# Reordering the front of a three-block language-model tower: warm-up matmuls, statistics one tile ahead, queries before the last values

## The reference

```python
tok = wte[input_ids]
Q = _layer_norm(tok, gamma, beta) @ W_proj.T            # 8 heads of 64
V = (tok @ W_val.T)
Q_store = Q[:, :, :-2, :] * arrow_mask                  # mask: id equals a link id
denom = jnp.maximum(arrow_mask.sum() * H, 1.0)
Q_erase = Q_store / norm(Q_store)
erase = einsum('bhip,bhiq->hpq', Q_erase, Q_erase @ value_traces) / denom
traces = 0.99 * (value_traces - erase) + 0.1 * einsum(Q_store, V_store) / denom
h = (shifted Q @ traces) @ W_out.T
# attention on _layernorm(h)
q, k, v = split(x @ W_qkv + b_qkv)
gw = softmax(gelu(v @ W_gp)); group_weight = gw @ gw.T
attn = softmax(q @ k.T * scale * group_weight)
out = ((1 - a) * attn + a * group_weight) @ v @ W_proj + b_proj
# then the experts on _layernorm(h)
```

## Time and profile before

| | us |
|---|---|
| median of 3 runs | 470.39 |
| lowest, highest | 470.22, 473.29 |
| the profiled execution | 471.55 |
| its span, first to last instruction | 469.7 |
| PE, PEld, DVE busy | 436.5, 360.1, 297.6 |
| ACT, POOL busy | 228.7, 145.8 |

### The profile page before, as it was taken

One profiled execution on the slowest core, in us unless ns is written; L12 is line 12 of the kernel. 1 busy time (PEld: TensorE's weight loads), 2 busy tenths in 40 slices (PEclk: granted clock), 3 DMA queues, 4 the chain that ended last, 5 costly groups with the idle time before them and its releaser, 6 DMA issues.

```text
span 469.7 us, 8294 instructions
## 1 busy us (share of the span) xinstructions
PE 436.5 (93%) x3086; PEld 360.1 (77%) x3086; DVE 297.6 (63%) x776; ACT 228.7 (49%) x415; POOL 145.8 (31%) x235
## 2 busy tenths in 40 slices
PE   5989998898698999999999989999999899999995
PEld 2667755697477888888888878889985576877895
DVE  6489872684935486667777586767765333543564
ACT  4568632598523535553432384887875321222220
POOL 5878500374100037220002393003451332212310
PEclk9999999999978999999999999999999999999999
DMA  3343000200000000500000000001809999999504
GB/s 95 109 133 99 5 2 0 102 1 29 1 1 0 1 0 1 201 3 0 1 0 1 1 2 0 1 1 39 365 20 420 391 367 374 372 377 387 170 18 134
DMA packets 14231, 49.64 MB, mean 106 GB/s; under 512 B 3504, under 2 KB 8528, under 8 KB 9968
## 3 DMA queue, kind: packets, MB, share of 16 engines
q1 hardware_dynamic: 7584, 43.21, 24.6%
q0 software_dynamic: 2912, 3.37, 2.6%
q10 hardware_dynamic: 3696, 2.54, 1.7%
HBM read 45.94 MB, written 3.15 MB: 104 GB/s over the span
## 4 chain that ended last, share of the span: by engine, by line
PE 67%; DMA 12%; DVE 12%; issue 3%; POOL 3%; ACT 2%; SPq 0%; POOLq 0%; ACTq 0%
DMA w1r<-in_p_w 10%; PE ps L888 10%; PE ps L934 8%; PE ps L1091 6%; PE ps L1032 3%; PE ps L870 3%; PE ps L1061 2%; PE ps L914 2%; PE ps L842 2%; DMA tok<-in_L_tok_wte,ints 2%; PE ps L915 2%; PE ps L918 2%; PE ps L916 2%; PE ps L917 2%; PE ps L843 2%
## 5 line engine op out<-in xcount | busy, mean ns | idle before, releaser
L888 PE MATMUL ps<-pr,et 128*128 128x192 f32 x256 | 48.1, 340 | 2.1 <-DVE et L1744 1.6
L888 PEld LDWEIGHTS ps<-pr,et 128*128 128x128 f32 x256 | 42.7, 194 | 5.4 <-ACT et L1313 3.1
L1091 PE MATMUL ps<-ys,ct 128*128 128x192 f32 x256 | 45.2, 330 | 1.1 <-DMA ys<-ys_dram 1.1
L1911 DVE TENSOR_TENSOR res<-ps,res 128x384 f32<-128x384 f32 x64 | 35.7, 558 | 14.6 <-PE ps L1091 10.1
L1091 PEld LDWEIGHTS ps<-ys,ct 128*128 128x128 f32 x256 | 41.2, 190 | 4.5 <-issue 2.7
L495 POOL TENSOR_SCALAR ve<-mv 128x1 f32<-128x1 f32 x32 | 12.1, 380 | 94.6 <-DVE mv L1759 53.3
L579 POOL DMA_DIRECT2D ys<-ys_dram x32 | 19.7, 619 | 69.4 <-DMA ys_dram<-ysb 67.8
L1302 ACT ACTIVATE scs<-ps,pr 128x1024 f32<-128x1024 f32 x16 | 17.9, 1116 | 37.8 <-PE ps L846 37.8
L1429 ACT ACTIVATE hs<-ps 128x384 f32<-128x384 f32 x16 | 7.9, 491 | 58.1 <-PE ps L1032 58.1
L1306 ACT ACTIVATE zz<-zz,nmx 128x1024 f32<-128x1024 f32 x16 | 18.4, 1152 | 27.3 <-DVE nmx L1738 27.0
L1902 DVE COPY ysb<-ps 128x192 f32<-128x192 f32 x16 | 5.7, 357 | 39.3 <-PE ps L1061 39.3
(11 more groups left out here) (318 smaller groups left out, 1202.4 us busy)
## 6 DMA issues: line engine op xcount, KB each, us to landing
w1r<-in_p_w SPq DMA_DIRECT2D x16, 1152.0 KB, 19.0
w2r<-in_p_w SPq DMA_DIRECT2D x16, 1152.0 KB, 18.6
ys_dram<-ysb ACTq DMA_DIRECT2D x16, 96.0 KB, 8.5
ys<-ys_dram POOLq DMA_DIRECT2D x32, 48.0 KB, 7.2
phT<-in_p_phi SPq DMA_DIRECT2D x1, 1024.0 KB, 4.7
wT<-in_p_qkv SPq DMA_DIRECT2D x1, 774.0 KB, 4.0
out<-res SPq DMA_DIRECT2D x3, 192.0 KB, 3.4
out<-res ACTq DMA_DIRECT2D x3, 192.0 KB, 3.8
```

What stands on the lines that cost most here:

```text
L888: last = mm(d[:, 0:D], et[:, k, :], pr[:, b * KT + k, 1:1 + D], start=(k == 0), stop=(k == KT - 1))
L1091: last = mm(bank(5 + q % 3)[:, h * D:(h + 1) * D], ct[:, u % 2, k + h, :], ys[:, t % YR, b, :], start=True, stop=True)
L1911: v.tensor_tensor(res[:, i:i + 2, :], bank(5 + q % 3)[:, 0:2 * D].rearrange("p (h d) -> p h d", h=2), res[:, i:i + 2, :], ALU.add).then_in ...
```

## The change

1. **Start of TensorE.** Nine 128x128 matmuls of ones run as soon as the ones are written. The eight small matmuls for beta by pairs leave; the count goes to bank 6. The wait for the count moves from the second `q_proj` to the third.
2. **Factors and gathers.** GpSimd computes the factors of tiles 1 and 2 apart and gathers up to tile i + 4 and not i + 6. The loop's pairs stay.
3. **Statistics.** VectorE takes `stats(1)` and `stats(2)` earlier, between the pieces of the weights. In the loop `ahead(s)` is gone: step s has `stats(s + 1)`, still behind `norms` and `erase_q`. The count's four small operations move into step 2.
4. **Beta by pairs** is made ahead of `prepare("kB2")` by four matmuls with one row of weights, and copied straight to wpn.
5. **B2 parts** take one VectorE instruction and not two.
6. **Queries.** `query(0)` to `query(3)` stand in the second loop behind the last four `value_proj`; two more behind it; the last two behind the first ten score matmuls. The group weights' half of the first scores waits alone for `gw_lo`. `norm_groups(1)` and the last two `q_lo` go behind `z_tile(0)`.

```diff
-            return bank(j if j < GTS else 4 + j - GTS)
+            return bank(3 + j if j < GTS else 4 + j - GTS)
+        QUERY_BANK = [0, 1, 2, 7, 5, 6, 7, 5]
@@ GpSimd
             gather(3)
+            front_factors(1, 2)
             gather(4)
-            front_factors(1, 3)
+            front_factors(2, 3)
             pool.wait_ge(m["mask_ready"], 1)
             masked(0)
-            gather(5)
-            gather(6)
             for i in range(1, NT):
-                if i + 6 < NX:
-                    gather(i + 6)
+                if i + 4 < NX:
+                    gather(i + 4)
                 masked(i)
                 if i % 2 and i + 2 < NT:
                     front_factors(i + 2, min(i + 4, NT))
@@ TensorE
+            pe.wait_ge(m["ones_ready"], 1)
+            for k in range(9):
+                mm(bank(2)[:, 0:P], ones[:], ones[:], start=True, stop=True)
...
-            for t in range(HP):
-                c, o = slice(t * P, (t + 1) * P), slice(2 + 2 * t, 4 + 2 * t)
-                mm(bank(3)[:, o], wpT[:, 0, c], betA, start=True, stop=False)
-                last = mm(bank(3)[:, o], wpT[0:DB, 1, c], betB, start=False, stop=True)
+            mm(bank(6)[:, 0:1], ones[:], msum[:], start=True, stop=True).then_inc(m["cnt_filled"], 1)
...
+            for t in range(HP):
+                mm(setup_bank("kB2")[:, 272 + 2 * t:274 + 2 * t], wpT[DB:DB + 1, 1, t * P:(t + 1) * P],
+                   ones[DB:DB + 1, 0:2], start=True, stop=True)
             prepare("kB2", at["kA"] + 1)
...
                 if 5 <= s:
                     value_proj(s - 5)
+                if s > NT:
+                    query(s - NT - 1)
...
-            for j in range(2 * QPS - 2):
+            for j in range(QPS, QPS + 2):
                 query(j)
             for j in range(GTS):
                 gw_T(j)
-            for j in range(2 * QPS - 2, 2 * QPS):
-                query(j)
@@ scores
                 if k == 0:
-                    pe.wait_ge(m["qpl_taken"], QPS * (b + 1))
-                    pe.wait_ge(m["gwT_taken"], GTS * (b + 1))
+                    pe.wait_ge(m["qpl_taken"], QPS * b + 2)
...
+                if i == 0:
+                    for j in range(QPS + 2, 2 * QPS):
+                        query(j)
+                if k == 0:
+                    pe.wait_ge(m["gwT_taken"], GTS * (b + 1))
@@ VectorE
-                    link(remainder(B2[DB:DB + 2, :], d[DB:DB + 2, 0:n], scale[2], B2[DB:DB + 2, :]))
-                    last = v.tensor_scalar(B2[DB:DB + 1, :], d[DB:DB + 1, 0:n], scale[3], None, ALU.mult)
+                    last = remainder(B2[DB:DB + 1, :], d[DB:DB + 1, 0:n], scale[2], B2[DB:DB + 1, :])
...
-            def ahead(s):
-                if s <= 4:
-                    return {2: [3, 4], 3: [5], 4: [6, 7]}.get(s, [])
-                return [s + 3] if s + 3 < NT else []
...
                 if 4 <= s:
                     norms(s - 4)
                     erase_q(s - 4)
-                for i in ahead(s):
-                    stats(i)
+                if 2 <= s < NT - 1:
+                    stats(s + 1)
+                if s == 2:
+                    count()
...
-            norm_groups(0)
             for j in range(2):
                 q_lo(j)
             shift_groups(1)
-            for j in range(2, QPS):
-                q_lo(j)
-            norm_groups(1)
-            for j in range(QPS, 2 * QPS - 2):
+            norm_groups(0)
+            for j in range(2, QPS + 1):
                 q_lo(j)
             for j in range(GTS):
                 gw_lo(j)
...
                     z_tile(s)
+                if s == 0:
+                    behind_first_scores()
```

More of the change, by code:

```diff
@@ L184, in build @@
         eyeP = sb("eyeP", [P, DT], where=front)
-        bpair = sb("bpair", [P, 2 * HP], where=front)
         r1 = sb("r1", [P, HP, DT], where=front)
@@ L634, in _ @@
             pe.wait_ge(m["mask_ready"], 1)
-            pe.wait_ge(m["ones_ready"], 1)
-            mm(bank(3)[:, 0:1], ones[:], msum[:], start=True, stop=True)
-            for t in range(HP):
-                c, o = slice(t * P, (t + 1) * P), slice(2 + 2 * t, 4 + 2 * t)
-                mm(bank(3)[:, o], wpT[:, 0, c], betA, start=True, stop=False)
-                last = mm(bank(3)[:, o], wpT[0:DB, 1, c], betB, start=False, stop=True)
-            last.then_inc(m["cnt_filled"], 1)
+            mm(bank(6)[:, 0:1], ones[:], msum[:], start=True, stop=True).then_inc(m["cnt_filled"], 1)
             def slots(b, s):
@@ L770, in value_proj, with query @@
                         vAh, vAl, vB1, vB2).then_inc(m["pr_filled"], 1)
+            def query(j):
+                blk, c0 = divmod(j, 2)
+                w = slice(P, XC) if c0 else slice(0, P)
+                if j < QPS:
+                    pe.wait_ge(m["x1_ready"], NT - QPS + j + 1)
+                    pe.wait_ge(m["h_taken"], NT - QPS + j + 1)
+                elif j < QPS + 2:
+                    pe.wait_ge(m["pr_taken"], NT - 1 + j - QPS)
+                else:
+                    pe.wait_ge(m["qpl_taken"], (QPS, QPS + 1)[j - QPS - 2])
+                d = query_bank(j)
+                b, n = half_of(blk)
+                mm(d, kAh[:, w], X1H[b][:, 0, n], start=True, stop=False)
+                mm(d, kAl[:, w], X1H[b][:, 0, n], start=False, stop=False)
+                mm(d, kAh[:, w], X1L[b][:, 0, n], start=False, stop=False)
+                mm(d, kB1[:, w], X1H[b][:, 1, n], start=False, stop=False)
+                mm(d, kB2[:, w], X1L[b][0:DB + 2, 1, n], start=False, stop=True).then_inc(m["qp_filled"], 1)
             pe.wait_ge(m["xl_ones"], 1 + NB)
@@ L1238, in query_hi @@
                 b, n = half_of(blk)
[L1239 removed]
+                sc.copy((qB if c0 else qAh)[b][:, n], query_bank(j)).then_inc(m["qph_taken"], 1)
             def gw_hi(j):
@@ L1282, in _ @@
                 gw_hi(j)
-            for j in range(2 * QPS - 2, 2 * QPS):
-                query_hi(j)
             def phi_parts(s):
@@ L1362, in _ @@
                     biased_scores(s)
+                if s == 0:
+                    for j in range(QPS + 2, 2 * QPS):
+                        query_hi(j)
                 if s == 1:
@@ L1688, in _, with behind_first_scores @@
                 gw_lo(j)
-            for j in range(2 * QPS - 2, 2 * QPS):
-                q_lo(j)
-            dve.wait_ge(m["alpha_exp"], 1)
-            link(v.tensor_scalar(aw[:, 2:3], aw[:, 1:2], 1.0, None, ALU.add))
-            link(v.reciprocal(aw[:, 2:3], aw[:, 2:3]))
-            link(v.tensor_tensor(aw[:, 3:4], aw[:, 1:2], aw[:, 2:3], ALU.mult))
+            q_lo(QPS + 1)
+            def behind_first_scores():
+                norm_groups(1)
+                for j in range(QPS + 2, 2 * QPS):
+                    q_lo(j)
+                dve.wait_ge(m["alpha_exp"], 1)
+                link(v.tensor_scalar(aw[:, 2:3], aw[:, 1:2], 1.0, None, ALU.add))
+                link(v.reciprocal(aw[:, 2:3], aw[:, 2:3]))
+                link(v.tensor_tensor(aw[:, 3:4], aw[:, 1:2], aw[:, 2:3], ALU.mult))
             def u_take(b):
```

75 lines of the change are left out of this document (35 added, 40 removed).

## The result

| | before | after |
|---|---|---|
| median, us (4 runs each, same chip) | 471.66 | 485.18 |
| lowest, highest | 470.22, 473.29 | 482.27, 485.85 |
| span of the profiled execution | 469.7 | 484.0 |

The ratio is 1.0274, with a 95% interval of 1.0213 to 1.0334: slower by 2.7%. The forecast was slower, 481.0 with a range of 473 to 489.

A forecast was written before the change was run, and what follows sets the result against it. It took TensorE, busy 436.5 of 469.7 us, as the bound, with VectorE nearly without slack in the front loop. Front +15.5, middle +0.6 and queries -5.7 made +10.4 on 470.4: 481 us, range 473 to 489.

The forecast's parts named there:

- The front loop: Front loop: VectorE waits 3.53 us for the factor chain in every odd step, pairs take 9.37 us; +15.5 us.
- The last stretch: End of the front loop, up to the low part of tile 15: 2.96 + 3.53 + 2.15, together 8.6 us.
- TensorE's share: Front loop, 26 to 62 us: TensorE's busy share falls from 0.97 to about 0.6.
- rival A: Front loop: the stalls are there and TensorE's clock falls in them; 490 us, more likely 486; chance 0.17.
- The start: Kernel start: first low parts at about 20.1 instead of 21.89 us; nine matmuls on ones cost nothing.
- The middle: Ahead of kB2: four matmuls add 1.04 us, a dropped VectorE operation saves 0.42; +0.6 us (0.3 to 1.7).
- The saving in vB2: vB2: one VectorE operation fewer may give 0.2 us, left out of the sum.
- The queries: Last value projections to first turn: queries made earlier bring the first turn to 141.3 us; -5.7 us (-3 to -8).
- the ring: Front loop: statistics, factors, normalization, high part and next low part wait on each other; 3.53 us per pair.
- B: Front loop: half of each wait is covered, a stall costs 1.7 us; 472 to 474 us; chance 0.11.
- C: Front loop: TensorE's 2.8 us still set the step and the queries decide; faster, 463.5 us; chance 0.07.
- D: Query section: gains nothing, since late last values move the softmax chain by 3.5 us; 486.5 us; chance 0.06.

The follow-up runs named there:

- g2_fillers: Changed kernel with filler matmuls on ones: seven ahead of the turn of each odd tile from 3 on, five ahead of nB2; 483.44 us.
- e2_before_stats_late: Kernel before with one edit: in the front loop, the statistics of tile s + 1 in step s, gathers unchanged; 491.43 us.
- h1_chain_longer: Changed kernel with GpSimd's power of the LayerNorm factors computed twice in a row; 489.65 us.
- e4_factors_single: Changed kernel with GpSimd's factors taken tile by tile in the loop, statistics still one tile ahead; 467.57 us.
- g1_no_warmup: e1_stats_as_before without the nine matmuls on ones; 464.55 us.
- e1_stats_as_before: Changed kernel with the order of statistics and gathers of the kernel before (three and six tiles ahead); 465.67 us.
- e3_before_queries: Kernel before with the query part of the change alone, with its banks; 464.55 us.
- b2_gather_later: Changed kernel, statistics three ahead from step 6, gathers five ahead, early single factors, beta matmuls moved to the front, tile 8's statistics behind XL of tile 4; 467.8 us.

## Why the prediction was right, point by point

**The front loop, right in mechanism and place, short by 2.1 us.** Predicted was a wait of 3.53 us in every second step and a pair of 9.37; measured 3.41 and 9.42 to 9.45. XL of tile 4 was put at 29.5 and came at 29.13. Tile 15 was put at 75.6 and came at 77.71. Two terms were too small. The first is a matter of size. The four pairs were put at 37.5 and took 67.73 - 29.13 = 38.60: one of them has the wrap of the first sequence in it, which the earlier trace rows don't show, 10.29 us from 48.00 to 58.29 and 9.71 in `g2_fillers`, where the clock stayed up. The second was wrongly made, and that its size came near is luck. The last stretch was put at 8.6 and took 9.98. Its sum, 2.96 + 3.53 + 2.15, has one wait for the whole chain and two steps; from tile 12 to tile 15 there are three steps, and no such wait: the factors of tile 15 want no tile behind it, ScalarE's high part of tile 13 stands ahead of `normalise(15)`, and that of tile 14 has a whole step of VectorE to hide behind. The idle times ahead of XL are 0.57, 1.16 and 0.61 us there. What fills the stretch is TensorE, which is the bound there and ran at its lower level for part of it; at the full level `e2_before_stats_late` shows 8.49, near the 8.6 but for another reason. TensorE's stretch by two us and one projection of after:

```profile
68.00:70.00 2.00, 2.00 (x16) 0.53 0.20 50
```

```profile
70.36 0.80 PE L595 MATMUL ps<-wpAh,XH 128*128 128x512 f32 x1
```

The same matmul takes 0.50 us in the next step (73.75). `h1_chain_longer` and `e4_factors_single` show that it is this chain and this pairing; before them it was only argued.

**TensorE's share**, predicted to fall from 0.97 to about 0.6, fell to 27.11/36 = 0.75. The number of matmuls fell to 0.60; the busy time did not follow, since they took longer at a granted clock of 0.86. That is under the 0.9 that I gave as the sign of rival A, so by my own sign A happened, in part. Its sum was wrong, though: it charged the lower clock to every pair, and `g2_fillers` shows that a wait of 3.4 us swallows it. What the clock did cost fell elsewhere: about 1.5 us in the last stretch, 0.6 in the wrap's pair, 1.7 in the middle.

**The start.** The lead was put at 1.8 us and was 2.3 to 2.9, and it was used up by the first uncovered chain, as predicted. That the nine matmuls cost and bring nothing in the front is shown by `g1_no_warmup`.

**The middle**, +0.6 predicted (0.3 to 1.7), +2.2 measured at its end, above the bound, and +1.7 with what the second loop gives back. The two terms that I named were right: four matmuls 0.98 (94.92 to 95.90, predicted 1.04), one VectorE operation less 0.46 (the lag goes from 18.56 to 18.10; predicted 0.42). The saving in vB2, which I left out at 0.2, is the 0.45 that comes back in the second loop: 19.78 to 19.33, where the same second operation (92.27, 0.41 us in before) is gone. What I missed is the product with wpn, 5.77 us against 4.09 before:

```profile
80.19 4.09 PE L739 MATMUL ps<-mm,wpn 128*66 128x192 f32 x24 [1.62 <-issue]
```

```profile
98.00:104.00 6.00, 5.71 (x24) 0.72 0.00 0
```

The first row is of before, the second of after. The wait ahead of it became shorter (1.16 and not 1.62), and yet the clock fell. `h1_chain_longer` and `e1_stats_as_before`, with the same instructions and the same wait of 1.16, take 4.09. So this loss belongs to no edit in the middle. Whether it depends on what went before or only on the execution isn't settled, since each kernel has one profile; a prediction from rows of before could not have placed it.

**The queries**, -5.7 predicted and -5.7 measured (19.3 to 13.6). The last pr copy came 2.1 us later than the lag of 19.3 there accounts for (predicted 2.3), the first z 7.1 earlier (7.2), and from the copy at 136.17 to the first turn it is 24.45 us (24). This term I left alone: behind the first turn another 1.6 us are won, because the granted clock stays up. After, then before:

```profile
160.00:168.00 8.00, 7.34 (x42) 1.00 0.00 0
```

```profile
148.00:152.00 4.00, 4.00 (x16) 0.57 0.00 0
```

And 2.2 us are lost at the last turn of the attention, where after waits 1.93 us for et (before 1.36) and then runs low:

```profile
293.00:296.00 3.00, 3.00 (x12) 0.57 0.00 0
```

**The sum.** +15.5, +0.6, -5.7 and nothing behind made +10.4. The terms measured in the two profiles are +17.6, +1.7 (2.2 less 0.5), -5.7, -1.6 and +2.2, together +14.2; the medians differ by 13.5. About 5.4 us of the terms are clock: 1.5 and 0.6 in the front, 1.7 in the middle, and of the last turn's 2.2 the 1.6 that its longer wait (0.57) doesn't explain. The prediction had none of it in its likeliest case, and 1.6 came back behind the first turn. The result of 485.18 lies inside the range but between my forecast's 479 to 484 and rival A's 486 to 490: the ring was right, and what it lacked is mostly A's clock, in other places than A had it. The clock terms are read off one execution of each kernel, and another one can have them otherwise.

**The rivals.** B (half of each wait covered) and C (TensorE sets the step) are out by the 3.41 us. D (the queries gain nothing) is out by `e3_before_queries`.

## What to carry to other kernels

Before a producer is moved closer to its consumer, count the steps between them by the consumer's unit: here a consumer that works by pairs wants the second tile of its pair two steps early, and one step ahead is none. What follows a wait in an engine's list decides whether it closes a ring; if the producer's next work waits for the consumer's, the whole chain is paid in each round (3.41 us here), and no engine is the bound. A gain in one part (1.2% in the queries) is seen only if the parts are run apart; the best kernels here, 464.55 us both, are the kernel before with the query part alone, and the changed kernel with the old statistics and without the matmuls on ones.

## What the runs showed of the hardware that I had not expected

The granted clock fell behind waits of about the same length in one execution and not in another. Ahead of the first turn TensorE waits 1.97 us in before and in after, and 1.98 in `e3_before_queries`; behind it the clock reads 0.57 in before (the earlier trace rows have 0.55 in one of these stretches) and 1.00 in after, and it stays up in `e3_before_queries` too, where seven of the turn's eight matmuls take 0.96 us. The product with wpn behind a wait of 1.16 us took 5.77 us in after and 4.09 in two other kernels. Inside the changed kernel's front loop it alternates. Once in each pair, ahead of the turn of a tile whose xh came late, TensorE stood idle for 1.68, 2.19 and 2.19 us at 27.83, 46.70 and 66.44, and the clock fell each time; in the two pairs between, its work at the lower level had shortened that wait to 0.67 and 0.20 us, and it stayed up. What tips it isn't settled by these runs. The Trainium skill (TensorE: Matmul & The Clock Gate, HAM oscillation) has the clock fall again in the wait between two bursts of matmuls. The front loop of after agrees in three pairs of five, and the rows above show that the wait's length alone doesn't say whether it will. A wait isn't always needed either: in the profiled executions of `e4_factors_single` and `b2_gather_later` the clock fell at 75 and 74 us, where TensorE had been busy without a break for over 5 us.

Clock regained in one place was lost in another: the fillers won 1.8 us by the first z, and 0.4 were left by the third. The medians moved by less than their spread, so the fillers' price and gain can't be told apart in the total.

A lower clock was nearly free where another chain set the pace: pairs of 9.42 to 9.45 us at a granted clock of 0.86 on average, and of 9.44 to 9.59 at 0.95 with the fillers, the pair with the wrap left aside.
